# Weighing the values of two chunks in every step of the wide attention, in place of four chunks in every second step

## The chip, the cores and the metric

One core of one Trainium2 chip runs the whole program. The metric is device time in microseconds of one execution, as the median of several runs. Engines are named as in the profile: PE is TensorE's matrix part, PEld its weight loads, DVE VectorE, ACT ScalarE, POOL GpSimd, SP SyncE.

## The reference

The program is a two-layer perceiver: cross attention on a context, self attention and experts, twice. The change touches only the first cross attention ("wide": 16 heads of 64, 4 batches, 256 queries, 4096 context rows of 256):

```
kv = context @ w_kv
k, v = jnp.split(kv, 2, axis=-1)
k = k.reshape(B, SK, NUM_HEADS, DIM_HEAD)
v = v.reshape(B, SK, NUM_HEADS, DIM_HEAD)
scores = jnp.einsum('bqhd,bkhd->bhqk', q * SCALE, k)
attn = jax.nn.softmax(scores, axis=-1)
out = jnp.einsum('bhqk,bkhd->bqhd', attn, v).reshape(B, SQ, INNER)
```

`out` is then multiplied with `w_out` and added to the stream. In the kernel the last einsum is called *weighing*: for 128 keys at a time (a chunk) the values are multiplied with the exponentials of the scores, and summed over the chunks in PSUM.

## The kernel before, in words

`wide_attention` (the loops stand on lines 549 to 568 for PE, 624 to 640 for ACT, 719 to 737 for DVE, 782 for POOL) goes through `G` = 32 groups, each one batch and one pair of heads. A group has `CH` = 32 chunks of 128 keys, taken two at a time: `ST` = 16 steps of a group, `LAST` = 512 steps in all. A step t on PE is, in program order:

- `weigh` (line 501), in odd t only, for the steps t-3 and t-2 together. One `weigh(u)` is four matmuls (two chunks, two heads), each with 64 columns of values as weights and 256 columns of exponentials streaming. They are plain fp32, and the trace has two records for each, so the two calls in a row are 16 records of L510. All of it accumulates in `ps_o`.
- `denominator` (L517) in the second step of a group: the ones times `acc`, the sum of the exponentials that POOL builds.
- `maximum` (L488): two matmuls on half of the rows of the array, 64 by 128, for the row maxima of the *next* group. DVE reduces them (L677).
- `scores(t)` (L530, L534): first four matmuls of form 64 by 128 for the low part, then four of the full form 128 by 128. They add to a bank of PSUM in which ACT has laid minus the maximum (`initial`, L605), and ACT takes the exponentials out of it (`exponents`, L613).
- in the last step of a group `turn_maximum` (L498), from which ACT builds `m_wide` (L594).
- in odd t `project_keys` (L449), six matmuls with 512 columns each, and in some steps `project_values` (L475), twelve with 256 columns. `V_STEPS` puts these mostly into even t; with two groups in a quad of 32 steps, only the steps 16 and 18 of a quad are even and without them. The first quad has none before step 20, and none are left in the last 17 steps, where keys and maxima have also ended.

The order on PE is written out by hand. What it waits for: `scores(t)` needs the two banks initialised, and there are three banks (`BANKS`), so ACT has to take two exponentials of step t-1 and lay one new bank after the scores of t-1 are ready, before `scores(t)` can start. `weigh(u)` needs the exponentials of step u (`exp_done`) and the values (`v_ready`). ACT may overwrite a slot of `probs` (a ring of `R` = 8 chunks) when it has been weighed (`pv_done`) and summed by POOL (`summed`). In every even step ACT takes the projected keys (L588) ahead of the exponentials, and DVE takes their low part (L666) after the maximum of that step.

Of the kernel before, what the change touches and what calls it, by code (L numbers as in the profile page):

```python
# [221 lines left out]
def wide_attention(nc, ctxT, w_kv, q_high, q_low, ctx_split, w_split, o_out, ident, ones):  # L222
# [15 lines left out]
    with nc.cleanup_on_exit(), ExitStack() as stack:  # L238
# [52 lines left out]
        def key_block(t):  # L291

            n = CG + (t + 3) // 2
            return n if t % 2 and n < G * CG else None

        def max_unit(t):

            n = t + 1
            return (1 + n // ST, n % ST // 2, n % 2) if 1 + n // ST < G else None

        def value_unit(t):

            for q in (t // 32, t // 32 + 1):
                if 1 <= q < QUADS and t - 32 * (q - 1) in V_STEPS:
                    return q, V_STEPS.index(t - 32 * (q - 1))
            return None
# [117 lines left out]
        def _(pe):  # L424
# [6 lines left out]
            def project_keys(kb):  # L431
                g, k = kb // CG, kb % CG
                if g == 0:
                    source = stage[k % 2]
                    pe.wait_ge(high_ready, k + 1)
                    pe.wait_ge(low_ready, k + 1)
                    if k == 0:
                        pe.wait_ge(first_ready, 1)
                else:
                    source = k_ctx[kb % 2]  # L440
                    pe.wait_ge(k_ctx_in[kb % 2], 16 * ((kb - CG) // 2 + 1))
                    if k == 0:
                        pe.wait_ge(wk_in[g % 2], 16 * ((g + 1) // 2))
                if kb:
                    pe.wait_ge(kl_ready, 2 * kb)
                n = 0
                for c in range(KD):
                    for part, of in ((0, 0), (0, 1), (1, 0)):
                        ins = pe.matmul(ps_k[:, :], w_k[g % 2][:, part, c, :], source[:, of, c, :],  # L449
                                        start=(n == 0), stop=(n == 3 * KD - 1))  # L450
                        n += 1
                ins.then_inc(kproj_done, 1)

            def project_values(q, hb, turns):
                vb = CG * q + hb // 2
                if q == 0:
                    source = stage[vb % 2]
                    pe.wait_ge(high_ready, vb + 1)
                    pe.wait_ge(low_ready, vb + 1)
                    if hb == 0:  # L460
                        pe.wait_ge(first_ready, 2)
                else:
                    source = v_ctx[vb % 2]
                    pe.wait_ge(v_ctx_in[vb % 2], 16 * ((vb - CG) // 2 + 1))
                    if hb == 0:
                        pe.wait_ge(wv_in, 32 * q)
                    pe.wait_ge(wide_ready, turns)
                if q or hb:
                    pe.wait_ge(v_ready, 2 * CG * q + hb)
                for i in range(2):  # L470
                    cols = slice((hb % 2 * 2 + i) * P, (hb % 2 * 2 + i + 1) * P)
                    n = 0
                    for c in range(KD):
                        for part, of in ((0, 0), (1, 0), (0, 1)):
                            ins = pe.matmul(ps_v[:, i * 256:(i + 1) * 256], source[:, of, c, cols], w_v[:, part, c, :],  # L475
                                            start=(n == 0), stop=(n == 3 * KD - 1))
                            n += 1
                ins.then_inc(vproj_done, 1)

            def maximum(g, k, half):  # L480
                if k == 0 and half == 0:
                    pe.wait_ge(q_in[g % 3], 48 * (g // 3 + 1))
                pe.wait_ge(kh_ready, (g * CG + k + 1) * 2)
                if g or k or half:
                    pe.wait_ge(m_taken, (g * CG + k) * 2 + half)
                for h in range(2):
                    r = slice(h * DH, (h + 1) * DH)
                    ins = pe.matmul(ps_m[:, h, :], qh[g % 3][r, h, half * P:(half + 1) * P],  # L488
                                    keys[g % 2][h][r, k * 512:(k + 1) * 512], start=True, stop=True)
                ins.then_inc(m_done, 1)  # L490

            def turn_maximum(g):
                pe.wait_ge(neg_ready, g + 1)
                pe.wait_ge(v_ready, 2 * CG + sum(value_unit(t) is not None for t in range(ST * g - 1)))
                for h in range(2):
                    for half in range(2):
                        col = h * SQ + half * P
                        ins = pe.matmul(ps_v[:, col:col + P], m_neg[:, 2 * half + h, :], ident[:, :], start=True, stop=True)  # L498
                ins.then_inc(mT_done, 1)

            def weigh(u):
                a, hb = u // ST, u % ST
                pe.wait_ge(exp_done, 2 * u + 2)
                pe.wait_ge(v_ready, 2 * CG * (a // 2) + hb + 1)
                if hb == 0 and a:
                    pe.wait_ge(o_copied, a)
                for c in (2 * hb, 2 * hb + 1):
                    for h in range(2):
                        col = a % 2 * P + h * DH
                        ins = pe.matmul(ps_o[h * DH:(h + 1) * DH, 0:SQ], values[:, c, col:col + DH],  # L510
                                        probs[:, c % R, h * SQ:(h + 1) * SQ], start=(c == 0), stop=(c == CH - 1))
                ins.then_inc(pv_done, 1)

            def denominator(a):
                pe.wait_ge(summed, (a + 1) * SUMS)
                for h in range(2):
                    ins = pe.matmul(ps_o[h * DH:(h + 1) * DH, SQ:2 * SQ], ones[:, 0:DH], acc[:, h * SQ:(h + 1) * SQ],  # L517
                                    start=True, stop=True)
                ins.then_inc(den_done, 1)

            def scores(t):
                a, c = t // ST, t % ST * 2
                n = 2 * t
                if c == 0:
                    pe.wait_ge(kl_ready, 2 * CG * (a + 1))
                pe.wait_ge(init_done, n + 2)
                for i in range(2):
                    for h in range(2):
                        r = slice(h * DH, (h + 1) * DH)
                        pe.matmul(ps_s[(n + h) % BANKS][:, i * SQ:(i + 1) * SQ], keys[a % 2][h][r, (c + i) * P:(c + i + 1) * P],  # L530
                                  ql[a % 3][r, :], start=False, stop=False, skip_group_check=True)
                for h in range(2):
                    for i in range(2):
                        ins = pe.matmul(ps_s[(n + h) % BANKS][:, i * SQ:(i + 1) * SQ], keys[a % 2][h][:, (c + i) * P:(c + i + 1) * P],  # L534
                                        qh[a % 3][:, h, :], start=False, stop=True, skip_group_check=True)
                    ins.then_inc(s_ready, 1)
# [11 lines left out]
            maximum(0, CG - 1, 1)  # L548
            for t in range(-3, LAST + 2):
                a, st = t // ST, t % ST  # L550
                if t % 2 and t >= 3:
                    weigh(t - 3)
                    weigh(t - 2)
                if st == 1 and t > 1:
                    denominator(a - 1)
                unit = max_unit(t)
                if t >= -1 and unit is not None:
                    maximum(*unit)
                if 0 <= t < LAST:
                    scores(t)  # L560
                if st == ST - 1 and a + 1 < G:
                    turn_maximum(a + 1)
                kb = key_block(t)
                if kb is not None:
                    project_keys(kb)
                unit = value_unit(t)
                if unit is not None:
                    project_values(*unit, turns=(t + 1) // ST + 1)
# [2151 lines left out]
```

## Time and profile before

| | |
|---|---|
| median of 3 runs | 4371.15 us (4368.67 to 4373.83) |
| the profiled execution | 4371.64 us, its span 4369.9 us |
| wide attention's main loop in it | scores from 158.1 to 2078.7 us |
| mean granted clock of TensorE | 0.952 of full speed |
| PE busy over the span | 3948.9 us (90%) |
| DVE, ACT, POOL busy | 2704.8, 2369.3, 1552.2 us |

The profile shows one execution. In its timeline of PE a line is a run of records of one kind; the time is the start of the first, the length reaches to the modelled end of the last. Matmuls are pipelined, so the length of a run overlaps with the next one: what a run costs PE is read from start to start.

### The profile page before, as it was taken

What the parts mean: (1) busy time and instruction counts of PE and PEld (TensorE: products, weight loads), DVE (VectorE), ACT (ScalarE), POOL (GpSimd) and SP (SyncE); (2) the same over time, 40 slices, a digit from 0 to 9 for tenths busy, and PEclk for the clock granted to TensorE, in tenths of its full rate; (3) what the DMA queues carried; (4) which work ended last, traced back from release to release, by engine and by line L of the source; (5) the groups of instructions that cost most, each with busy time, mean ns of one, the idle gap of its engine ahead of it and who ended that gap; (6) DMA issues with size and microseconds to landing.
All of it is one profiled execution on the core that took longest, in us unless ns stands there. A gap on an engine that the chain in (4) does not pass through costs nothing. (4 is left out here: it accounts for less than half of the span.)

```text
span 4369.9 us, 74948 instructions
## 1 busy us (share of the span) xinstructions
PE 3948.9 (90%) x26760; PEld 2746.4 (63%) x26760; DVE 2704.8 (62%) x4112; ACT 2369.3 (54%) x4373; POOL 1552.2 (36%) x1229
## 2 busy tenths in 40 slices
PE   5899999999999999998677976999999999676599
PEld 2677777777777777776446965555555555343365
DVE  4766666666666666663264124677776777476666
ACT  2677777777777777776142112555555566444111
POOL 1566666666666666666022003000000000033000
PEclk9999999999999999999788987999999999888799
DMA  5777767777677666662203647544444422100011
GB/s 194 273 252 252 248 241 260 256 256 250 239 265 252 247 232 222 232 224 80 78 10 121 266 171 261 151 156 137 142 148 141 120 58 65 31 2 5 18 37 42
DMA packets 232703, 724.77 MB, mean 166 GB/s; under 512 B 44557, under 2 KB 129805, under 8 KB 163725
## 3 DMA queue, kind: packets, MB, share of 16 engines
q1 hardware_dynamic: 229664, 711.78, 47.8%
q0 software_dynamic: 2688, 8.39, 0.5%
q8 instruction: 211, 3.46, 0.3%
q14 instruction: 140, 1.14, 0.1%
HBM read 625.70 MB, written 94.37 MB: 165 GB/s over the span
## 5 line engine op out<-in xcount | busy, mean ns | idle before, releaser
L752 POOL TENSOR_TENSOR wa_acc<-wa_acc,wa_probs 128x512 f32<-128x512 f32 x960 | 1246.5, 1298 | 525.1 <-ACT wa_probs L613 444.9
L677 DVE TENSOR_REDUCE wa_mx<-wa_ps_m 128x2 f32<-128x1024 f32 x512 | 626.6, 1224 | 486.1 <-PE wa_ps_m L488 485.9
L613 ACT ACTIVATE wa_probs<-wa_ps_s 128x512 f32<-128x512 f32 x1024 | 556.3, 595 | 525.5 <-PE wa_ps_s L534 520.2
L1204 ACT ACTIVATE na_probs<-na_ps_s 128x512 f32<-128x512 f32 x1024 | 564.1, 599 | 377.8 <-PE na_ps_s L1108 372.4
L1256 DVE TENSOR_REDUCE na_mx<-na_ps_m 128x1 f32<-128x512 f32 x1024 | 643.0, 681 | 186.8 <-PE na_ps_m L1093 185.8
L605 ACT ACTIVATE wa_ps_s<-wa_m_wide 128x512 f32<-128x512 f32 x1024 | 575.7, 605 | 1.0
L510 PE MATMUL wa_ps_o<-wa_probs,wa_values 128*64 128x256 f32 x4096 | 505.3, 389 | 0.0
L1093 PE MATMUL na_ps_m<-na_keys,na_q 98*128 98x512 f32 x1024 | 425.8, 424 | 41.7 <-DVE na_mx L1256 28.6
L1108 PE MATMUL na_ps_s<-na_q,na_keys 100*128 100x512 f32 x1024 | 429.8, 427 | 2.4 <-ACT na_probs L1204 1.6
L449 PE MATMUL wa_ps_k<-wa_k_ctx,wa_w_k 128*128 128x512 f32 x1488 | 388.6, 396 | 0.0
L475 PE MATMUL wa_ps_v<-wa_w_v,wa_v_ctx 128*128 128x256 f32 x2880 | 382.5, 282 | 0.0
L534 PE MATMUL wa_ps_s<-wa_qh,wa_keys 128*128 128x256 f32 x2048 | 381.2, 309 | 0.0
L510 PEld LDWEIGHTS wa_ps_o<-wa_probs,wa_values 128*64 128x64 f32 x4096 | 274.0, 138 | 148.5 <-issue 5.3
L475 PEld LDWEIGHTS wa_ps_v<-wa_w_v,wa_v_ctx 128*128 128x128 f32 x2880 | 363.1, 191 | 2.4
L666 DVE TENSOR_TENSOR wa_keys<-wa_ps_k,wa_keys 64x512 fp32r<-64x512 f32 x512 | 352.7, 689 | 18.5 <-ACT wa_keys L588 2.5
L1330 POOL TENSOR_TENSOR na_k_low<-na_k_masked,na_k_high 128x512 fp32r<-128x512 f32 x64 | 84.3, 1320 | 726.9 <-ACT na_k_high L1186 726.0
L534 PEld LDWEIGHTS wa_ps_s<-wa_qh,wa_keys 128*128 128x128 f32 x2048 | 275.7, 189 | 70.4 <-issue 0.6
L588 ACT ACTIVATE wa_keys<-wa_ps_k 64x512 fp32r<-64x512 f32 x512 | 300.8, 588 | 28.3 <-PE wa_ps_k L449 22.2
L449 PEld LDWEIGHTS wa_ps_k<-wa_k_ctx,wa_w_k 128*128 128x128 f32 x1488 | 263.3, 189 | 43.8 <-issue 0.4
L1108 PEld LDWEIGHTS na_ps_s<-na_q,na_keys 100*128 100x128 f32 x1024 | 190.7, 189 | 151.2 <-issue 65.0
L1093 PEld LDWEIGHTS na_ps_m<-na_keys,na_q 98*128 98x128 f32 x1024 | 195.1, 191 | 143.9 <-DVE na_mx L1256 107.8
L1120 PE MATMUL na_ps_o<-na_probs,na_v_all 128*17 128x256 f32 x4096 | 280.4, 382 | 0.9 <-ACT na_probs L1204 0.9
(329 smaller groups left out, 5108.6 us busy)
## 6 DMA issues: line engine op xcount, KB each, us to landing
wa_k_ctx<-ctx_split SPq DMA_DIRECT2D x248, 1024.0 KB, 5.1
wa_v_ctx<-ctx_split SPq DMA_DIRECT2D x120, 1024.0 KB, 5.7
na_ctx<-ctx_split SPq DMA_DIRECT2D x56, 1024.0 KB, 6.9
na_keys<-k_rows SPq DMA_DIRECT2D x192, 256.0 KB
ctx_split<-wa_stage SPq DMA_DIRECT2D x32, 1024.0 KB, 9.7
wa_land<-in_ctxT SPq DMA_DIRECT2D x32, 512.0 KB, 10.3
ge_w_b<-in_w_rows SPq DMA_DIRECT2D x8, 2048.0 KB
k_rows<-na_k_high SPq DMA_DIRECT2D x64, 256.0 KB, 2.3
```

The lines of the kernel that those rows point to most:

```text
L449: ins = pe.matmul(ps_k[:, :], w_k[g % 2][:, part, c, :], source[:, of, c, :], start=(n == 0), stop=(n == 3 * KD - 1))
L475: ins = pe.matmul(ps_v[:, i * 256:(i + 1) * 256], source[:, of, c, cols], w_v[:, part, c, :], start=(n == 0), stop=(n == 3 * KD - 1))
L510: ins = pe.matmul(ps_o[h * DH:(h + 1) * DH, 0:SQ], values[:, c, col:col + DH], probs[:, c % R, h * SQ:(h + 1) * SQ], start=(c == 0), stop= ...
L534: ins = pe.matmul(ps_s[(n + h) % BANKS][:, i * SQ:(i + 1) * SQ], keys[a % 2][h][:, (c + i) * P:(c + i + 1) * P], qh[a % 3][:, h, :], start ...
L605: act.activation(ps_s[n % BANKS][:, :].rearrange("p (c n) -> p c n", c=2), of_head, ACT.Copy).then_inc(init_done, 1)
L613: act.activation(probs[:, c % R:c % R + 2, h * SQ:(h + 1) * SQ], ps_s[n % BANKS][:, :].rearrange("p (c n) -> p c n", c=2), ACT.Exp).then_i ...
L677: dve.tensor_reduce(mx[:, half, :, k], ps_m[:, :, :], AX.X, ALU.max).then_inc(m_taken, 1)
L752: pool.tensor_tensor(acc[:, :], acc[:, :], probs[:, c % R, :], ALU.add).then_inc(summed, 1)
L1093: pe.matmul(ps_m[n % RM][:, :], q[a % 3][0:MROWS, j // 2, (j % 2) * P:(j % 2 + 1) * P], keys[a % 2][0:MROWS, u * 512:(u + 1) * 512], start ...
L1108: pe.matmul(ps_s[n % RS][:, :], keys[a % 2][0:ROWS, c * P:(c + 1) * P], q[a % 3][0:ROWS, :, :].rearrange("p h n -> p (h n)"), start=True, ...
L1204: act.activation(probs[:, n % RP, :], ps_s[n % RS][:, :], ACT.Exp).then_inc(exp_done, 1)
L1256: dve.tensor_reduce(mx[:, j, u:u + 1], ps_m[n % RM][:, :], AX.X, ALU.max).then_inc(m_taken, 1)
```

## The change

Before, PE weighed in odd t only, and then the steps t-3 and t-2. Now it weighs in every t from 2 on, and then the step t-2 alone. The number of matmuls, their operands and the order of the accumulation in `ps_o` stay. Nothing changes on the other engines.

```
             for t in range(-3, LAST + 2):
                 a, st = t // ST, t % ST
-                if t % 2 and t >= 3:
-                    weigh(t - 3)
+                if t >= 2:
                     weigh(t - 2)
                 if st == 1 and t > 1:
                     denominator(a - 1)
```

## Rows read from the trace of the kernel before

**Rows 1.** Windows: length, busy us (count) of PE, PEld, DVE, ACT, POOL, clock, DMA, GB/s.
```profile
388.60:1966.20 1577.60, 1574.71 (x11544) 1186.13 (x11544) 1051.98 (x1191) 1137.52 (x2127) 1046.76 (x807) 1.00 0.69 245
2034.40:2085.00 50.60, 39.54 (x244) 23.90 (x242) 1.57 (x3) 28.04 (x54) 37.45 (x30) 0.83 0.01 3
```
**Rows 2.** Waits from 200 to 2000 us: total us, times, longest us.
```profile
PEld wa_ps_m L488 <- issue: 166.2, 447, 0.4
...
PEld wa_ps_s L530 <- issue: 12.1, 30, 0.4
```
**Rows 3.** Timeline of PE, one pair of steps: start us, length us, group.
```profile
1001.49 1.53 PE L449 MATMUL wa_ps_k<-wa_k_ctx,wa_w_k 128*128 128x512 f32 x6
1002.95 0.50 PE L488 MATMUL wa_ps_m<-wa_keys,wa_qh 64*128 64x512 f32 x2
1003.29 0.40 PE L530 MATMUL wa_ps_s<-wa_ql,wa_keys 64*128 64x256 f32 x4
1003.62 0.74 PE L534 MATMUL wa_ps_s<-wa_qh,wa_keys 128*128 128x256 f32 x4
1004.20 1.60 PE L475 MATMUL wa_ps_v<-wa_w_v,wa_v_ctx 128*128 128x256 f32 x12
1005.73 1.95 PE L510 MATMUL wa_ps_o<-wa_probs,wa_values 128*64 128x256 f32 x16
1007.61 0.50 PE L488 MATMUL wa_ps_m<-wa_keys,wa_qh 64*128 64x512 f32 x2
```
**Rows 4.** The same L510 group, windows beginning at its fifth and eleventh record.
```profile
1006.21 1.47 PE L510 MATMUL wa_ps_o<-wa_probs,wa_values 128*64 128x256 f32 x12
...
1006.86 0.82 PE L510 MATMUL wa_ps_o<-wa_probs,wa_values 128*64 128x256 f32 x6
```
**Rows 5.** Timeline of PE, an even step without values.
```profile
822.67 0.40 PE L530 MATMUL wa_ps_s<-wa_ql,wa_keys 64*128 64x256 f32 x4
...
823.00 0.74 PE L534 MATMUL wa_ps_s<-wa_qh,wa_keys 128*128 128x256 f32 x4
...
823.67 1.95 PE L510 MATMUL wa_ps_o<-wa_probs,wa_values 128*64 128x256 f32 x16
...
825.89 0.40 PE L530 MATMUL wa_ps_s<-wa_ql,wa_keys 64*128 64x256 f32 x4
```
**Rows 6.** Timeline of PE and ACT behind a turned maximum.
```profile
814.96 1.64 ACT L605 ACTIVATE wa_ps_s<-wa_m_wide 128x512 f32<-128x512 f32 x3
...
815.60 0.51 PE L488 MATMUL wa_ps_m<-wa_keys,wa_qh 64*128 64x512 f32 x2
...
816.22 0.50 PE L530 MATMUL wa_ps_s<-wa_ql,wa_keys 64*128 64x256 f32 x4
...
816.65 0.74 PE L534 MATMUL wa_ps_s<-wa_qh,wa_keys 128*128 128x256 f32 x4
```
**Rows 7.** Timeline before a turned maximum: DVE's last values, PE's turn.
```profile
869.29 0.69 DVE L673 COPY wa_values<-wa_ps_v 128x512 f32<-128x512 f32 x1
...
871.06 0.60 PE L498 MATMUL wa_ps_v<-g_ident,wa_m_neg 128*128 128x128 f32 x4
```
**Rows 8.** Timeline of the last group of heads, PE and POOL.
```profile
2031.04 0.60 PE L517 MATMUL wa_ps_o<-wa_acc,g_ones 128*64 128x256 f32 x4
...
2031.83 1.28 POOL L749 TENSOR_TENSOR wa_acc<-wa_probs 128x512 f32<-128x512 f32 x1 [2.84 <-PE wa_ps_o L517]
...
2039.13 0.74 PE L534 MATMUL wa_ps_s<-wa_qh,wa_keys 128*128 128x256 f32 x4
...
2041.30 0.50 PE L530 MATMUL wa_ps_s<-wa_ql,wa_keys 64*128 64x256 f32 x4 [1.43 <-ACT wa_ps_s L605]
...
2047.99 3.63 PE L510 MATMUL wa_ps_o<-wa_probs,wa_values 128*64 128x256 f32 x16
...
2068.02 11.17 POOL L752 TENSOR_TENSOR wa_acc<-wa_acc,wa_probs 128x512 f32<-128x512 f32 x8 [1.54 <-ACT wa_probs L613]
...
2083.56 0.65 PE L517 MATMUL wa_ps_o<-wa_acc,g_ones 128*64 128x256 f32 x4 [1.67 <-POOL wa_acc L752]
```

More of the change, by code:

```diff
@@ L550, in _ @@
                 a, st = t // ST, t % ST
-                if t % 2 and t >= 3:
-                    weigh(t - 3)
+                if t >= 2:
                     weigh(t - 2)
```

## The prediction

> **What bounds the kernel now.** I read the windows first. In the middle of wide attention, 388.6 to 1966.2 us, PE is busy for 1574.7 of 1577.6 us at the full clock, DVE for 1052, ACT for 1138 and POOL for 1047 [rows 1]. So PE's order of work sets the time there, and an edit pays only what it adds to or takes from PE from start to start. The waits confirm this: PEld has only two kinds of idle time, 0.37 us ahead of nearly every `maximum` (447 times) and 0.4 us in 30 cases ahead of the low scores [rows 2]. The second kind comes once per group. In the last group the picture changes: the clock is 0.83 and POOL is the busiest after PE, 37.5 of 50.6 us with a PE busy for 39.5 [rows 1]. What follows wide attention is not touched and is carried over.
>
> The timeline of one pair of steps shows how it adds up [rows 3]. Odd step, from `scores` on: keys to `maximum` 1002.95 - 1001.49 = 1.46 (1.48 in most pairs, taken below as equal to it), `maximum` to low scores 0.34, low to high scores 0.33, high scores to the next group 0.58. Even step: values to weighing 1.53, weighing to `maximum` 1007.61 - 1005.73 = 1.88. A pair with values takes 7.37 us, one without 5.93, one period after the other alike to 0.01 us.
>
> **The price of one more group.** The change moves half of each L510 group (four source matmuls, eight records) out of the even interval into the odd one, between keys and `maximum`. The matmuls are the same in number, so what counts is what a group costs besides them. The two narrower windows start at 1006.21 and 1006.86, with three pairs of records between them: 0.65 / 3 = 0.216 us a pair [rows 4]. Eight pairs are 1.73; the group takes 1.88 to the next start [rows 3]. So each group carries 0.15 us of its own. Half a group takes 4 x 0.216 + 0.15 = 1.02. The way in has to be looked at too. High scores reach weighing in 0.67 [rows 5] against 0.58 to a group of their own form [rows 3]: entering costs 0.09. But the keys now leave for `maximum`, which is a change of form as well, so a way of that kind is already in their 1.46. I put keys to weighing equal to keys to `maximum`.
>
> - Odd interval: +1.02 us. Even interval: -4 x 0.216 = -0.86. Pair: +0.15.
> - Pairs in which PE sets the pace: odd steps 1 to 493, 247 of them: 247 x 0.15 = **+37 us**. Bounds: a way in or out shorter by 0.05 gives +25; 0.20 a group gives +49. The trace doesn't show keys followed by weighing; I take the middle: the nearest row, scores to weighing, has an entry of 0.09, and low to high scores, again a change of form, fits into 0.33.
>
> The Trainium skill, page "TensorEngine Tiling (Array Packing)", section "Key Properties", says that changing the tiling mode, not just the tile, drains TensorE. It gives no time for it. By that rule the added group is one drain more per pair, and the trace agrees (0.15 us a group).
>
> **What the odd interval gives back.** ACT must be done with two exponentials and one new bank before the next `scores`. Where nothing else fills PE, high scores to the next low scores takes 2041.30 - 2039.13 = 2.17 us, and such a `scores` also loads late, 0.43 instead of 0.33 [rows 6, 8]. Three places follow:
>
> - Behind a turned maximum ACT has a copy and three banks to do [rows 6]. PE goes from `maximum` to low scores in 0.62 and on in 0.43, instead of 0.34 and 0.33 [rows 3, 6]: 0.38 too long. These are the 30 waits in rows 2. The 1.02 us of weighing now lie ahead of this `maximum` and behind the turn, so ACT has that much more time, and the wait should go: 30 x 0.38 = **-11 us**. What comes due next there is ACT's taking of the keys ahead of the exponentials; the scores come 0.7 us later than before, which covers it. Bounds: 0 to -11.
> - An even step without values now has only 0.67 + 1.02 before `maximum`, so low scores would load at about 1.79 us after the high scores, with ACT ready at 2.17. The step becomes ACT's: 2.17 + 0.43 = 2.60 in place of 825.89 - 822.67 = 3.22 [rows 5], which is -0.62 and not -0.86: +0.24. Steps 18 of 14 quads and 7 of the first quad (the others of its even steps have the denominator or a cold start): 21 x 0.24 = **+5 us**. Steps with values have 1.53 more on PE and no stall; step 16 has the denominator, 0.53 more, which is just enough. Bounds: +3 to +10, if ACT starts later there.
> - DVE frees the bank that the turn needs at 869.98 (869.29 + 0.69), and PE turns at 871.06: 1.08 us of slack [rows 7]. DVE's chain starts from the `maximum` of that even step, and PE now comes 0.86 sooner behind it. 0.2 is left. If it were gone, each 0.1 would cost 31 x 0.1 = 3 us. I take 0.
>
> **The last group.** From the denominator of group 30 to that of group 31 takes 2083.56 - 2031.04 = 52.5 us [rows 8]. Here odd steps have scores only and wait 1.4 us for ACT, while all the weighing stands in the even ones, where one group of 16 takes 3.63 us, at the half clock (1.2 GHz), to which PE had fallen after such waits [rows 8]; the stretch has 0.83 on the mean [rows 1]. With half a group in each step, PE has 0.57 + 0.10 + 1.02 us of work inside the 2.17 that ACT takes anyway. A step is then 2.60, two are 5.2, and POOL is later than that: 11.17 / 8 = 1.40 us an addition, 5.6 a pair of steps [rows 8]. POOL's 31 operations take 43.4, the first starts 0.8 behind the denominator (2031.83 - 2031.04), and I allow 0.6 for one wait at the start: 44.8 instead of 52.5. Another 0.86 comes from the even interval ahead of the denominator, whose odd partner waits for ACT anyway. **-8.5 us.** Bounds: if the clock still falls in this stretch, two steps of PE cost about 7 (3.63 for the weighing, twice the 1.0 of scores and a half more) and nothing is won: 0 to -9.
>
> **Sum.** 37 - 11 + 5 - 8.5 = +22.5 us on the profiled execution's 4371.64: 4394. It lies 0.5 above the median, which changes nothing at this size.
>
> **Rivals.**
>
> - *A boundary between forms is free, because the weights of the next group are loaded under the running one.* Then the 0.15 is something that stays with the sixteen records, and the other terms stand: -11 + 5 - 8.5 = -14.5, 4357 us. For it: inside the L510 group the pairs follow each other every 0.216 us, loads and all [rows 4]. Against it: PEld sits idle 0.37 us ahead of `maximum` in 447 cases with nothing to wait for [rows 2], and weighing ends 0.15 late [rows 3, 4]. It decides if a group costs under 0.06 us (14.5 / 247). 0.08. The Trainium skill, "TensorE: Matmul & The Clock Gate", section "Part 2: What happens when you issue a matmul", says that PE's reorder window pulls weight loads ahead of matmuls in flight, which taken by itself gives this rival; the trace shows that it doesn't hold across these forms.
> - *The group costs what I say, and nothing is given back*: ACT's chain slides with PE behind the turns, and the last group stays at the half clock in parts. 37 + 5 = +42, 4414 us; with the turn recovered and only the last group not, 4402. For it: ACT takes keys first, and the clock of 0.83 shows how readily it falls there [rows 1]. Against it: the added 1.02 us lies exactly where ACT is late. 0.12 for the first form.
> - *Spreading the work evens PE's load, and waits vanish which the trace hides in the 1.48 between keys and `maximum` or in the 0.34 after it.* 0.02 on 247 pairs is -5, and with a group at 0.10 the sum is +5, 4377: no change that can be told. 0.10.
>
> **Chances.** My forecast 0.70 (4394), free boundary 0.08, nothing given back 0.12, evened out 0.10. About 0.2% (8.7 us) can be told from no change. Faster 0.08, same 0.12 (the third rival and a little of the forecast's low end), slower 0.80. The range reaches from the third rival's side, 4376, to just short of the second, 4411.
>
> **What the changed kernel's profile would show.** Keys to weighing 1.48, then 1.02 to `maximum`, in odd steps, and 1.02 in even ones; pairs with values at 7.52 instead of 7.37. No idle time of PEld ahead of L530 behind a turn, `maximum` to scores 0.34 there. Step 18 of a quad 2.60 long, with ACT named. The last group some 45 us from denominator to denominator, POOL without gaps, the clock near 1. The waits ahead of `maximum` in equal number, and idle time ahead of L510 in twice as many places. I would be wrong if the odd interval grew by other than 1.02, or if ACT's exponentials (needed one step sooner for the even u) held up L510.

## The result

| | median, us | lowest and highest | ratio to before, 95% interval |
|---|---|---|---|
| before | 4371.15 | 4368.67 to 4373.83 (5 runs) | |
| changed kernel | 4391.15 | 4384.17 to 4395.83 (5 runs) | 1.0045 (1.0031 to 1.006) |
| forecast | 4394 | 4376 to 4411 | 1.005 |

The changed kernel is 20 us slower, with the interval clear of 1, and the forecast was 22.5 us on the profiled execution. The profiled execution of the changed kernel took 4384.17 us (span 4382.4), the quickest of its five, so its span shows only 12.5 us more. That is why the stage has to be read and not the span.

Three stretches of the stage, each from one low-score group to another or to a denominator, read from the timelines of both kernels:

| stretch | before | after | difference | forecast |
|---|---|---|---|---|
| first quad (steps 0 to 31) | 158.14 to 267.25 | 154.10 to 268.08 | +4.9 | +4.3 |
| the next 14 quads (to step 480) | 267.25 to 1966.25 | 268.08 to 1992.22 | +25.1 | +26.3 |
| step 480 to the last denominator | 1966.25 to 2083.56 | 1992.22 to 2101.29 | -8.2 | -8.4 |

Together +21.8 us. The forecast column spreads the terms of the prediction's sum over the stretches: 0.15 a pair, -0.38 a turn, +0.24 a bare even step (one without values), -8.5 for the last group; unrounded they add up to +22.2. At each border between two stretches the half group added ahead of it (+0.86) and the wait of 0.28 that goes there (-0.28) are counted ahead of the border, and the half group taken away stands behind it. What lies ahead of the stage (4.0 us less) and behind it (2281.1 instead of 2286.3 us) is the same work in both kernels. In a second profiled execution of the changed kernel, shown below as e8_again, the stage begins at 158.68, ends its last denominator at 2105.32, and the rest takes 2285.7 us. The 9 us by which the first execution was quicker outside the stage are thus no effect of the change.

### The profile page after: what moved, and what is told of

Same layout as the page of the kernel before. It is cut to its first block and busy times, and to the rows that moved or that the text cites. A ratio compares the mean times of both kernels' runs of the same rounds, so it can differ in the third digit from the quotient of the medians.

```text
span 4382.4 us, 74948 instructions
## 1 busy us (share of the span) xinstructions
PE 3964.4 (90%) x26760; PEld 2708.7 (62%) x26760; DVE 2704.4 (62%) x4112; ACT 2368.3 (54%) x4373; POOL 1548.5 (35%) x1229
## 5 line engine op out<-in xcount | busy, mean ns | idle before, releaser
L510 PE MATMUL wa_ps_o<-wa_probs,wa_values 128*64 128x256 f32 x4096 | 554.9, 392 | 0.0
L510 PEld LDWEIGHTS wa_ps_o<-wa_probs,wa_values 128*64 128x64 f32 x4096 | 248.3, 136 | 191.0 <-ACT wa_probs L612 50.6
```

## The profile after

The form of a matmul is the part of the array that it takes, rows by columns, as `128*128` or `64*128` in the lines. The lines of ACT, DVE and POOL have numbers lower by one in the changed kernel. The timeline of PE in it, a pair of plain steps, as [rows 3] shows it of before:

```profile
1034.67 1.53 PE L449 MATMUL wa_ps_k<-wa_k_ctx,wa_w_k 128*128 128x512 f32 x6
1036.13 1.08 PE L510 MATMUL wa_ps_o<-wa_probs,wa_values 128*64 128x256 f32 x8
1037.15 0.50 PE L488 MATMUL wa_ps_m<-wa_keys,wa_qh 64*128 64x512 f32 x2
1037.49 0.40 PE L530 MATMUL wa_ps_s<-wa_ql,wa_keys 64*128 64x256 f32 x4
1037.83 0.74 PE L534 MATMUL wa_ps_s<-wa_qh,wa_keys 128*128 128x256 f32 x4
1038.40 1.60 PE L475 MATMUL wa_ps_v<-wa_w_v,wa_v_ctx 128*128 128x256 f32 x12
1039.93 1.08 PE L510 MATMUL wa_ps_o<-wa_probs,wa_values 128*64 128x256 f32 x8
1040.95 0.50 PE L488 MATMUL wa_ps_m<-wa_keys,wa_qh 64*128 64x512 f32 x2
```

There are now two L510 groups of eight records, each 1.02 us from its start to the `maximum` behind it (1037.15 - 1036.13, 1040.95 - 1039.93), together 2.03 against 1.88 for the one group of sixteen [rows 3]. Keys to weighing is 1.46, where keys to `maximum` was 1.46: the way out of the keys costs the same into either form. No other number of the pair has moved.

What the 0.15 us of a group consists of can be read in the kernel before, where some groups are followed by one of their own form:

```profile
997.94 1.95 PE L510 MATMUL wa_ps_o<-wa_probs,wa_values 128*64 128x256 f32 x16
999.72 0.60 PE L517 MATMUL wa_ps_o<-wa_acc,g_ones 128*64 128x256 f32 x4
...
1038.37 1.55 PE L449 MATMUL wa_ps_k<-wa_k_ctx,wa_w_k 128*128 128x512 f32 x6
1039.75 1.59 PE L475 MATMUL wa_ps_v<-wa_w_v,wa_v_ctx 128*128 128x256 f32 x12
```

Weighing reaches the denominator, of its own form, in 1.78 us, and `maximum`, of another, in 1.88. Keys reach the values, of their own form, in 1.38, and `maximum` in 1.48 in most pairs. High scores reach keys or values in 0.58 and weighing in 0.67. So a change of form costs 0.09 to 0.10 us in each. Of the 0.15, some 0.10 is the change of form on the way out; 0.05 is there without one (1.78 against 1.73 for eight pairs).

The loads show where this happens, though their idle time is no measure of the cost. Of the waits from 200 to 2000 us in the changed kernel (total us, times, longest us) these are PE's own (`issue` names a wait for nothing that the profile shows):

```profile
PEld wa_ps_m L488 <- issue: 180.4, 469, 0.4
PEld wa_ps_o L510 <- ACT wa_probs L612: 47.4, 134, 0.4
PEld wa_ps_o L510 <- issue: 26.2, 73, 0.4
...
PEld wa_ps_s L530 <- ACT wa_ps_s L604: 4.9, 16, 0.3
```

Before, that list had no idle time ahead of L510, and 30 waits ahead of L530 [rows 2]. Now 207 of the L510 groups, those behind the keys, are entered with the loads idle for some 0.35 us. Behind the values the loads are idle for 0.13 us in both kernels, too short for the list. The 134 put down to ACT are a trap: ACT's exponentials for such a group were ready 3.0 to 4.2 us before, and the same group in the same place starts 1.46 behind the keys, like a `maximum`. The releaser is only the last event that the group's first load had asked for. The 30 issue waits ahead of L530 are gone, and 16 others have come. The next two readings show both.

The turned maximum in the changed kernel, as in [rows 6]:

```profile
822.97 1.64 ACT L604 ACTIVATE wa_ps_s<-wa_m_wide 128x512 f32<-128x512 f32 x3
823.63 0.63 PEld L510 LDWEIGHTS wa_ps_o<-wa_probs,wa_values 128*64 128x64 f32 x8 [0.36 <-issue]
...
824.64 0.50 PE L488 MATMUL wa_ps_m<-wa_keys,wa_qh 64*128 64x512 f32 x2
...
824.98 0.40 PE L530 MATMUL wa_ps_s<-wa_ql,wa_keys 64*128 64x256 f32 x4
...
825.31 0.74 PE L534 MATMUL wa_ps_s<-wa_qh,wa_keys 128*128 128x256 f32 x4
```

ACT's three banks (822.97 to 824.61) are laid while PE weighs. `maximum` to low scores is 0.34 instead of 0.62 and low to high scores 0.33 instead of 0.43: the 0.38 us are back.

An even step without values, as in [rows 5]:

```profile
831.26 0.42 PEld L530 LDWEIGHTS wa_ps_s<-wa_ql,wa_keys 64*128 64x128 f32 x4
831.50 0.40 PE L530 MATMUL wa_ps_s<-wa_ql,wa_keys 64*128 64x256 f32 x4
...
831.83 0.74 PE L534 MATMUL wa_ps_s<-wa_qh,wa_keys 128*128 128x256 f32 x4
...
832.50 1.08 PE L510 MATMUL wa_ps_o<-wa_probs,wa_values 128*64 128x256 f32 x8
...
834.00 0.30 PEld L530 LDWEIGHTS wa_ps_s<-wa_ql,wa_keys 64*128 64x128 f32 x4 [0.30 <-ACT wa_ps_s L604]
834.00 0.51 PE L530 MATMUL wa_ps_s<-wa_ql,wa_keys 64*128 64x256 f32 x4
...
834.44 0.54 PEld L534 LDWEIGHTS wa_ps_s<-wa_qh,wa_keys 128*128 128x128 f32 x4
```

High to low scores takes 2.17 us (834.00 - 831.83), ACT's own time in [rows 8], and the wait names ACT's bank. The other 0.10 of the predicted 0.25 shows one group on: low to high scores is 0.44. The two low scores differ in their loads: at 831.26 the first load runs 0.24 us ahead of the first matmul, at 834.00 both start together.

The last group, from denominator to denominator, in the changed kernel, with POOL's additions in it:

```profile
2056.19 0.60 PE L517 MATMUL wa_ps_o<-wa_acc,g_ones 128*64 128x256 f32 x4
...
2058.91 42.33 POOL L751 TENSOR_TENSOR wa_acc<-wa_acc,wa_probs 128x512 f32<-128x512 f32 x30 [0.65 <-ACT wa_probs L612]
...
2101.30 1.12 PE L517 MATMUL wa_ps_o<-wa_acc,g_ones 128*64 128x256 f32 x4 [4.86 <-POOL wa_acc L751]
```

45.1 us instead of 52.5 [rows 8]. POOL does its last thirty additions without a gap, and PE waits 4.86 us for them at the end.

## The experiments

Two families: take single parts of the change (e1 to e3, e7), and add boundaries or a fill without moving cover (e4 to e6).

**e1_both, e2_turns, e3_tail: only what should pay.**

```
# e2_turns
                if t % 2 and t >= 3:
                    if t % ST != 1 or t == 1:
                        weigh(t - 3)
                    weigh(t - 2)
                elif t % ST == 0 and t > 0:
                    weigh(t - 2)
# e3_tail: the same with "if t <= LAST - ST" and "elif t >= LAST - ST"
# e1_both: both conditions
```

> Only the single step of weighing right behind each turned maximum, the rest as before. Theory (a group costs 0.15, the wait of 0.38 goes): -7 us, quad of 32 steps 121.35 - 0.46 = 120.9. Rival (ScalarE's chain slides along, the wait stays): +5 us, quad 121.65. Rival (boundary is free): -12 us, quad 120.6.

> Only the last group's steps weigh one step each, the rest as before. Theory (the last group becomes GpSimd's, 1.40 us an addition, clock near full): denominator to denominator 45 in place of 52.5 us, total about -8.5 us with the interval ahead of it. Rival (the clock falls all the same): 50 to 53 us and 0 to -2 us.

> Weighs as the kernel before does (two steps together, in odd steps), except where the weighing moved ahead of a maximum fills a wait for ScalarE: one step alone right behind each turned maximum, and in every step of the last group. If a group of weighing costs 0.15 us of its own and the waits are given back: 31 x (0.15 - 0.38) = -7 us behind the turns and -8.5 us in the last group, so about 4356 us, 0.9964 of before. If nothing is given back, 31 x 0.15 = +5 us, about 4376. If boundaries are free, -12 - 8.5 = -20 us.

| | median, us | ratio, 95% interval | expected |
|---|---|---|---|
| e2_turns | 4362.96 | 0.9982 (0.9973 to 0.9991) | -7 us |
| e3_tail | 4361.42 | 0.9977 (0.9968 to 0.9986) | -8.5 us |
| e1_both | 4353.55 | 0.9958 (0.9944 to 0.9972) | -15.5 us |

Before took 4371.57 us in these comparisons (median), so the three are 8.6, 10.2 and 18 us faster. The ratios' intervals hold the expected -7, -8.5 and -15.5. They shut out the rivals in which nothing is given back. The profiled stage of e1_both, up to the last denominator, is 15.5 us shorter than that of before (1909.9 against 1925.4). On time alone they hardly shut out a free boundary at the turns (-12 us); the timeline of e2_turns does:

```profile
806.97 0.41 PE L530 MATMUL wa_ps_s<-wa_ql,wa_keys 64*128 64x256 f32 x4
807.30 0.74 PE L534 MATMUL wa_ps_s<-wa_qh,wa_keys 128*128 128x256 f32 x4
807.88 1.05 PE L498 MATMUL wa_ps_v<-g_ident,wa_m_neg 128*128 128x128 f32 x8
808.69 1.63 PE L449 MATMUL wa_ps_k<-wa_k_ctx,wa_w_k 128*128 128x512 f32 x6
810.25 1.08 PE L510 MATMUL wa_ps_o<-wa_probs,wa_values 128*64 128x256 f32 x8
811.26 0.50 PE L488 MATMUL wa_ps_m<-wa_keys,wa_qh 64*128 64x512 f32 x2
811.60 0.40 PE L530 MATMUL wa_ps_s<-wa_ql,wa_keys 64*128 64x256 f32 x4
```

The one added group takes 1.01 us, of which four pairs are 0.86, and `maximum` to scores is 0.34. A quad takes 120.90 us in e1_both and 120.96 in e2_turns instead of 121.36: 0.46 and 0.39 less, with 2 x (0.15 - 0.38) = -0.46 expected. Fourteen quads of e2_turns are thus 5.5 us shorter. Another 3.3 come behind step 480, and not by the turns alone: step 496 is 0.8 us shorter, the interval whose partner waits for ACT anyway, and in its last group one group of sixteen fewer ran slow (step 498 takes 2.98 instead of 4.52 us). In e3_tail the last group takes 45.13 us at a granted clock of 1.00. e1_both keeps both gains of the change and leaves out its cost. It is faster than before and than the changed kernel.

**e4_around: one group more per pair, no cover moved.**

```
                if t % 2 and t >= 3:
                    weigh(t - 3)
                ...                      # denominator, maximum
                if t % 2 and t >= 3 and st != 1:
                    weigh(t - 2)
```

In the steps with a denominator both stay together.

> Both steps are still weighed in the odd step, but one ahead of the maximum and one behind it. No work moves from one interval between scores to the other, so ScalarE's cover is the same; only groups and changes of form are added, one group per pair. Theory (each group 0.15 of its own, and 0.09 to enter it, since maximum to low scores was no change of form): a plain pair 7.37 + 0.24 = 7.6 us, 256 x 0.24 = +61 us, about 4432. Rival (boundaries are free, what the change cost was lost cover): 0 us, pair 7.37. Rival (every group 0.15 whatever lies beside it): +38 us.

4444.45 us, ratio 1.0164 (1.0148 to 1.0179): +73 us. The free boundary is out, and so is the flat price of 0.15 a group. My 0.24 was too small as well. The timeline of its PE:

```profile
857.38 0.50 PE L530 MATMUL wa_ps_s<-wa_ql,wa_keys 64*128 64x256 f32 x4
857.81 0.74 PE L534 MATMUL wa_ps_s<-wa_qh,wa_keys 128*128 128x256 f32 x4
...
862.64 1.08 PE L510 MATMUL wa_ps_o<-wa_probs,wa_values 128*64 128x256 f32 x8
863.65 0.50 PE L488 MATMUL wa_ps_m<-wa_keys,wa_qh 64*128 64x512 f32 x2
864.08 1.08 PE L510 MATMUL wa_ps_o<-wa_probs,wa_values 128*64 128x256 f32 x8
865.10 0.50 PE L530 MATMUL wa_ps_s<-wa_ql,wa_keys 64*128 64x256 f32 x4
```

A pair is 865.10 - 857.38 = 7.72 us, 0.35 above 7.37. Of it 0.15 is the group's own, 0.09 the way from `maximum` into it (0.43 where `maximum` to scores was 0.34), and 0.10 stands one group on: low scores that come straight behind weighing reach the high scores in 0.43 (857.81 - 857.38) instead of 0.33. That third part I had left out. Fourteen pairs of a quad are split so, 14 x 0.35 = 4.9, and its quad takes 126.19, 4.84 more.

**e5_maxlate: changes of form without any group of weighing.**

```
                if t >= -1 and unit is not None and (t % 2 == 0 or t < 0):
                    maximum(*unit)
                if 0 <= t < LAST:
                    scores(t)
                if t > 0 and unit is not None and t % 2:
                    maximum(*unit)
```

> Weighing as before; in odd steps the maximum is issued behind the scores instead of ahead of them (form 64 by 128 between high scores and keys, both 128 by 128). No group of weighing is added, but a pair has two changes of form more: high scores to maximum and maximum to keys, where it had none, and keys still go into another form, the low scores. Theory (the price is that of a change of form, about 0.10 each): a plain pair 7.37 + 0.2 = 7.55 us or some more, up to 7.8 if the loads of the maximum are late too. Rival (only weighing, with its plain fp32 and its waits, pays for a boundary): 7.37 us.

4474.3 us, where before took 4375.73 (median) beside it: one execution, +99 us. Its PE, from an odd step's low scores to the next even step's:

```profile
868.76 0.50 PE L530 MATMUL wa_ps_s<-wa_ql,wa_keys 64*128 64x256 f32 x4
869.19 0.74 PE L534 MATMUL wa_ps_s<-wa_qh,wa_keys 128*128 128x256 f32 x4
869.86 0.49 PE L488 MATMUL wa_ps_m<-wa_keys,wa_qh 64*128 64x512 f32 x2
870.29 1.67 PE L449 MATMUL wa_ps_k<-wa_k_ctx,wa_w_k 128*128 128x512 f32 x6
871.89 0.50 PE L488 MATMUL wa_ps_m<-wa_keys,wa_qh 64*128 64x512 f32 x2
```

Each of four places takes 0.09 to 0.14 more than in [rows 3]: low to high scores 0.43 instead of 0.33, high scores to the next group 0.67 instead of 0.58, out of `maximum` 0.43 instead of 0.34, keys to `maximum` 1.60 instead of 1.46 to 1.48. So the price is not peculiar to weighing: only the first of the four places has weighing beside it. The sum, 0.41, makes a pair 7.78 us (its quad is 6.5 us longer, 16 x 0.41), at the upper end of what I expected. The 0.2 of the low end counted the two changes of form, but not that the low scores now lie behind weighing, and the keys behind `maximum`, and start without loads made ahead. With one execution the total has no interval; the reading rests on the timeline.

**e6_warm: is it the clock in the last group?**

```
def fill():
    for n in range(6):
        pe.matmul(ps_k[:, :], w_k[1][:, 0, n % 2, :], k_ctx[1][:, 0, n % 2, :], start=True, stop=True)
...                              # at the end of step t
                if t % 2 and t > LAST - ST:
                    fill()
```

> The kernel before with six matmuls of 512 columns added in each odd step of the last group, into a bank nobody reads any more; they fill TensorE's wait for ScalarE and compute nothing. Theory that the clock is what the last group loses: it stays at full speed, a group of 16 records takes 1.88 instead of up to 3.6 us, a pair 2.6 + 3.0 = 5.6 us, denominator to denominator about 45 to 46 us, -6 us. Rival (what the change gave there was the even spreading, not the clock): the fill costs or gives nothing, 52 us.

4364.45 us, ratio 0.9977 (0.9967 to 0.9986): the kernel is faster with 54 matmuls more, 48 of them ahead of the last denominator. By the medians that is 11 us, and by the interval 6 to 14. The windows from denominator to denominator (columns as in [rows 1]), first of before, then of e6_warm:

```profile
2031.04:2083.56 52.52, 40.81 (x255) 24.90 (x251) 3.50 (x3) 30.09 (x58) 39.42 (x31) 0.84 0.01 3
```

```profile
2034.90:2080.18 45.28, 43.75 (x302) 29.00 (x298) 3.52 (x3) 29.88 (x57) 39.69 (x31) 1.00 0.01 4
```

and of the changed kernel:

```profile
2056.19:2101.29 45.10, 34.34 (x254) 20.38 (x250) 3.56 (x3) 30.93 (x60) 39.45 (x31) 1.00 0.01 4
```

The fill keeps the clock at 1.00 (2.4 GHz), and a group of sixteen takes its 1.88 again:

```profile
2044.71 1.95 PE L510 MATMUL wa_ps_o<-wa_probs,wa_values 128*64 128x256 f32 x16
2046.59 0.50 PE L530 MATMUL wa_ps_s<-wa_ql,wa_keys 64*128 64x256 f32 x4
```

Before, five of the seven even steps from 498 to 510 took 4.5 to 4.7 us and two took 2.98; in e6_warm all seven take 2.97. In e6_warm and in the changed kernel the stretch ends with POOL (some 39.5 us of additions in 45). What the change gains there is what the clock took. Spreading the work and the fill both keep the clock at 1.00, and either leads to the same bound. In the trace of e6_warm the step ahead of the stretch (496), before the first fill, took 1.5 us longer than before, so that from step 480 on 5.7 us are won and not 7.2; what the medians have beyond that no trace accounts for.

**e7_bare and e8_again: the steps that lose their cover.**

```
                bare = t < 20 or (t % 32 in (18, 19) and t < LAST - ST)
                if t >= 2 and not (bare and t % 2 == 0 and t % ST):
                    if bare and t % 2 and t >= 3 and t % ST != 1:
                        weigh(t - 3)
                    weigh(t - 2)
```

> The changed kernel, but the 22 pairs of steps whose even step has no value projection (8 in the first quad, one in each of 14 others) weigh two steps together as the kernel before. Theory (there the moved work uncovers ScalarE, and the pair pays 0.15 for the group and 0.25 for the wait): each such pair 5.93 in place of 6.34 us, quad of 32 steps 123.15 - 0.41 = 122.7, first quad 3 us shorter, -9 us against the changed kernel. Rival (only the group counts): -0.15 x 22 = -3 us, quad 123.0.

> The changed kernel once more, beside the others on one chip: +20 us against before, as the stage's own rows give +22 (theory) and not +12 as the profiled execution's total has it (rival: the sum of the terms is too large).

e7_bare took 4381.04 us (ratio 1.0025, 1.0014 to 1.0035) and the changed kernel beside it 4388.58 (1.0043, 1.0029 to 1.0057): 7.5 us apart, with 9 expected and 3 by the rival. The two intervals overlap, so the stage's rows have to decide. A quad takes 122.71 in e7_bare against 123.13, the expected 0.4, and the first quad 111.29 against 113.67, 2.4 less where 3 were expected (from step 3 on 98.83 against 101.66, 2.8 less; the first three steps vary from run to run, as said below). The step in question in e7_bare:

```profile
828.74 0.74 PE L534 MATMUL wa_ps_s<-wa_qh,wa_keys 128*128 128x256 f32 x4
829.41 1.95 PE L510 MATMUL wa_ps_o<-wa_probs,wa_values 128*64 128x256 f32 x16
831.29 0.50 PE L488 MATMUL wa_ps_m<-wa_keys,wa_qh 64*128 64x512 f32 x2
831.63 0.40 PE L530 MATMUL wa_ps_s<-wa_ql,wa_keys 64*128 64x256 f32 x4
```

`maximum` to scores is 0.34 again, with 0.49 in the changed kernel. The repeated changed kernel stands 18 us above before, by the ratio +19 of +13 to +25.

## Why the prediction was right, point by point

- *A group costs 0.15 us of its own.* 1.02 for half a group, twice in a pair; a pair 7.51 to 7.52 us. Right to 0.01, and 247 pairs carry it. Over the 14 quads a plain pair grew by 0.12 to 0.15, mostly 0.14 us, which is the greater part of why they lost 25.1 and not 26.3. Keys to weighing, which no row of before showed, is 1.46 as put.
- *Behind the turns 0.38 comes back.* Right in both parts, the wait and the faster low scores; e2_turns shows it alone.
- *Even steps without values become ACT's.* Right: 2.17 from high to low scores, +0.25 a step with the slower group behind; e7_bare takes it back.
- *Slack of DVE ahead of the turn.* Put at nothing, and it costs nothing: of the 1.08 us 0.41 are left, twice the 0.2 forecast (DVE's copy ends at 820.84, PE turns at 821.25), and high scores to the turn is 0.58 in the changed kernel (820.67 to 821.25 in its timeline), as elsewhere.
- *The last group is POOL's.* 45.1 us against 44.8 put, and -8.2 against -8.4 for the stretch. The reason given, the half clock, is shown by e6_warm. The 3.63 us that the prediction gives for a group of sixteen is one of the slow ones; two of seven ran at full speed there.
- *What was off.* The first quad lost 4.9 us and not 4.3. It has 8 bare steps and not the 7 I counted (+0.25). The rest lies in its first three steps, in which the clock still changes: 12.3 us (12.0 in e8_again) instead of 11.6, where kernels with the same work as before in these steps took 10.0 (e2_turns) to 12.5 (e7_bare). From step 3 on the quad lost 4.2 us in both profiled executions of the changed kernel, which is what the terms give for the fifteen odd and fourteen even steps in it. And the idle time of PEld ahead of L510 that I forecast "in twice as many places" was in no place of the list before, and in 207 after.
- *What was thin.* The reading of why a boundary costs: I had one price for the group and one for the entry. e4 and e5 show a third part, 0.1 us in the group behind, which didn't enter this sum only because in the changed kernel each weighing is still followed by `maximum` or the denominator and not by scores. That the sum came out without it is luck of this order of work.

The free boundary, the one rival that ended faster, had 0.08. All of e4, e5 and the pair of the changed kernel speak against it. The Trainium skill, "TensorEngine Tiling (Array Packing)", section "Key Properties", says that changing the tiling mode drains TensorE. The timelines here agree, with 0.09 to 0.10 us at each change of form that they let one compare.

## What to carry to other kernels

Before you even out an engine's work by cutting a group in two, count the changes of matmul form that the cut adds and price each from the start-to-start times of a timeline, where the busy time shows nothing (in a window from 400 to 2000 us PE is busy for all 1600, in the changed kernel as in e1_both). Where the order is written out by hand, look for the few places in which another engine is late, and cut there only: 31 cuts behind the turned maxima and 8 more in the last steps gave 18 us, where cutting at all 256 places cost 20. An engine that idles in short pieces can also lose its clock: here waits of 1.4 us for ACT came with a granted clock of 0.84, and filling them with useless matmuls made the stretch 7.2 us shorter. So look at the granted clock of such a stretch by itself.

## What the runs showed of the hardware that I had not expected

- A group of four matmuls of 64 by 128 takes 0.33 us to the next group behind a `maximum` of the same form, and 0.43 us behind a change of form or a wait. In the slower starts the first load and the first matmul begin together (834.00), in the others the load runs 0.20 to 0.24 us ahead (831.26 and 831.50). That the 0.10 us is this missing lead is my reading; no run changes the lead alone.
- Adding 48 matmuls of 512 columns to a stretch made it 7.2 us shorter (52.5 to 45.3 us); the granted clock stayed at 1.00 instead of 0.84.
- A change of form costs 0.09 to 0.10 us from start to start wherever these timelines have the same group with and without one behind it.
